# Choosing the experts tile by tile inside the graph layers, a third buffer for late one-hots, and the last projection ahead of the last pair

## The reference

```python
xn = _layernorm(x)
# graph layer: h = xn @ W; agg = segment_sum(norm * h[src], dst) + dinv^2 * h
#              h = layernorm(agg + b) * gamma + beta; relu(0.5 * h + 0.5 * xn)
# attention:   linear attention of all nodes, q = elu(q) + 1, one context for all; projected
x = x + _L0_gnn_ref(xn, ...) + _L0_mix_ref(xn[None], ...)[0]
# experts:     logits = x @ gate_w + gate_b; top 2; softmax of the two; relu(x @ w1 + b1) @ w2 + b2
#              y = x + weighted sum of the two experts; layernorm
x = x + _L0_ffn_ref(_layernorm(x)[None], ...)[0]
return x
```

## Time and profile before

| | us |
|---|---|
| median of 3 runs | 1805.78 |
| lowest and highest of them | 1800.36, 1808.45 |
| the profiled execution | 1800.89 |
| its span | 1799.1 |
| TensorE's matmuls busy | 1490.5 (83%) |
| GpSimd busy | 1065.6 (59%) |
| VectorE busy | 983.1 (55%) |

### The profile page before, as it was taken

How to read it: one execution, slowest core, us unless ns; L and a number is a source line. 1 busy time by engine, 2 the same in 40 slices (tenths; PEclk the granted TensorE clock), 3 DMA queues, 4 the chain that set the end, 5 groups by cost and what they waited for, 6 DMA issues and landing times. The chain is left out here.

```text
span 1799.1 us, 34047 instructions
## 1 busy us (share of the span) xinstructions
PE 1490.5 (83%) x7872; PEld 1211.9 (67%) x7873; DVE 983.1 (55%) x3365; ACT 531.1 (30%) x1463; POOL 1065.6 (59%) x1116
## 2 busy tenths in 40 slices
PE   7999778777978786977887779873499999999987
PEld 4676566565757565755765557652289989988976
DVE  8999466534466453742755347266833333343457
ACT  3444422111211121211211112110055555555523
POOL 2332477777777777777777777760045545545545
PEclk9999879986978898898889979876699999999989
DMA  8010533333333333333333333337432233254266
GB/s 277 28 36 24 164 103 106 106 103 105 104 105 103 104 104 105 102 105 105 103 103 104 105 102 105 104 101 144 114 110 77 72 118 94 73 182 131 70 233 232
DMA packets 105305, 200.76 MB, mean 112 GB/s; under 512 B 24384, under 2 KB 59840, under 8 KB 105248
## 3 DMA queue, kind: packets, MB, share of 16 engines
q0 software_dynamic: 48336, 132.17, 25.3%
q1 hardware_dynamic: 56624, 67.29, 12.2%
q10 hardware_dynamic: 288, 0.66, 0.1%
HBM read 166.44 MB, written 33.60 MB: 111 GB/s over the span
## 5 line engine op out<-in xcount | busy, mean ns | idle before, releaser
L786 POOL DMA_INDIRECT ring<-table,staged x784 | 746.1, 952 | 242.5 <-issue 229.4
L1061 PE MATMUL bank<-ring,hots 128*128 x1372 | 325.0, 392 | 50.3 <-SPq L775 50.3
L1061 PEld LDWEIGHTS bank<-ring,hots 128*128 128x128 f32 x1372 | 266.0, 196 | 100.6 <-issue 63.6
L1458 POOL DMA_INDIRECT got_x<-rows,at_x x114 | 110.2, 967 | 201.9 <-DVE at_x L1576 178.5
L1061 PE MATMUL bank<-ring,late_hots 128*128 x388 | 138.5, 506 | 98.2 <-SPq L775 89.6
L1553 PEld LDWEIGHTS bank<-xT,w 128*128 128x128 f32 x1696 | 207.1, 193 | 15.4 <-issue 10.2
L1553 PE MATMUL bank<-xT,w 128*128 128x128 f32 x1696 | 208.3, 276 | 8.6 <-issue 8.6
L1526 ACT ACTIVATE hT<-bank,b 128x128 f32<-128x128 f32 x424 | 155.7, 367 | 181.4 <-PE bank L1553 156.9
L1561 PE MATMUL bank<-w,hT 128*128 128x256 f32 x848 | 201.1, 380 | 2.3 <-DVE y L1618 2.2
L1061 PEld LDWEIGHTS bank<-ring,late_hots 128*128 128x128 f32 x388 | 90.2, 248 | 140.4 <-issue 126.5
L871 DVE TENSOR_SCALAR hots<-iota_t,edge_l 128x128 f32<-128x128 f32 x686 | 181.8, 363 | 1.8
(11 more groups left out here) (278 smaller groups left out, 2287.4 us busy)
## 6 DMA issues: line engine op xcount, KB each, us to landing
w<-in_w SPq DMA_DIRECT2D x32, 512.0 KB, 4.9
ring<-table,staged POOLq DMA_INDIRECT x784
got<-spread SPq DMA_DIRECT2D x11, 1024.0 KB, 8.1
rows<-xn SPq DMA_DIRECT2D x1, 6272.0 KB, 28.6
out<-out_c SPq DMA_DIRECT2D x12, 512.0 KB, 3.9
xt<-in_x_cols SPq DMA_DIRECT2D x11, 512.0 KB, 3.5
table<-xn SPq DMA_DIRECT2D x6, 896.0 KB, 6.5
x<-in_x SPq DMA_DIRECT2D x4, 896.0 KB, 11.2
```

The costliest lines, as they stand in the source:

```text
L786: pool.indirect_dma_start(out=ring[:, j, :], out_offset=None, in_=a.table, in_offset=bass.IndirectOffsetOnAxis(ap=staged[:, half, col:col ...
L1061: last = nc.tensor.matmul(agg, hot[:, k, :], two[:, k, :], start=False, stop=False)
L1458: pool.indirect_dma_start(out=got[:, n, :], out_offset=None, in_=a.rows, in_offset=bass.IndirectOffsetOnAxis(ap=at[:, n:n + 1], axis=0)).t ...
```

## The change

1. Top two in the layers. In turn t VectorE takes the top two of tile t - 6 (`top_two`, ten operations of 16 columns, behind `x1` and ahead of the wait for the tile's sum), TensorE ranks and counts that tile a turn later in the bank of the gate's product, and VectorE adds the counts so far (`m.run`) to its ranks and writes them over its logits. This is done for tiles 0 to 43 (`ROUTED`). `route` treats the five tiles left: operations of 80 columns, one count matmul and one rank matmul, five chained adds of 16 columns. The one-hots are kept in 16 bits. The shares are worked out behind the places.
2. `late_hots` has a third buffer: a tile's second later pair is built into it without a wait. A third later pair would still wait.
3. The output sum of the last tile (48) is made ahead of its last pair, with its halved input in `cur`, and not in turn 49.
4. Turns 6 and 7 are written out instead of looped. `rows_i`, `xT` and `hT` lie in memory of other tiles, and `places`, `list`, `lists` and `which` are allocated in `moe`.

```diff
+def top_two(dve, c, m, t, score, pick, rest, both):
+    down = m.const[:, C_DOWN:C_DOWN + E]
+    of = tile(m.logits, t, E)
+    for k in range(2):
+        best, one = tile(m.share, t, 2)[:, k:k + 1], tile(m.one[:, k], t, E)
+        c.add(dve.reduce_max(best, of, axis=AX.X))
+        c.wait()
+        settle(dve, m)
+        c.add(dve.scalar_tensor_tensor(score, of, best, down, ALU.is_equal, ALU.mult))
+        c.wait()
+        settle(dve, m)
+        c.add(dve.reduce_max(pick, score, axis=AX.X))
+        c.wait()
+        settle(dve, m)
+        c.add(dve.tensor_scalar(one, down, pick, None, ALU.is_equal))
+        c.wait()
+        settle(dve, m)
+        if k == 0:
+            c.add(dve.scalar_tensor_tensor(rest, one, -3e38, of, ALU.mult, ALU.add))
+            c.wait()
+            settle(dve, m)
+        of = rest
+    return dve.tensor_tensor(both, tile(m.one[:, 0], t, E), tile(m.one[:, 1], t, E), ALU.add)
...
                 with dve.If(end < last):
                     weighted(0, end)
                     with dve.If(end + 1 < last):
-                        with dve.Fori(end + 1, last) as pair:
+                        weighted(2, end + 1)
+                    with dve.If(end + 2 < last):
+                        with dve.Fori(end + 2, last) as pair:
                             dve.wait_ge(freed, pair + CREDIT)
                             settle(dve, m)
                             weighted(0, pair)
...
+                if routed(t, 6):
+                    top_two(dve, Count(dve, chain_top, (t - 6) * CHAIN_TOP, CHAIN_TOP), m, t - 6, score[:], pick[:], rest[:],
+                            m.both[:, n, :]).then_inc(both_ok, 1)
...
+                    if routed(t, 7):
+                        dve.tensor_tensor(tile(m.logits, t - 7, E), rank_ps, m.run[:, n, :], ALU.add)
+                        dve.tensor_tensor(m.run[:, o, :], total_ps, m.run[:, n, :], ALU.add)
...
+                    if routed(t, 7):
+                        pe.wait_ge(both_ok, t - 6)
+                        nc.tensor.matmul(rank_ps, m.tri, m.both[:, 1 - n, :], start=True, stop=True)
+                        done = nc.tensor.matmul(total_ps, m.ones, m.both[:, 1 - n, :], start=True, stop=True)
...
-                if on(t, 1):
...
+                if on(t, 1) and not (isinstance(t, int) and t == LAST + 1):
+                    summed_up(t - 1, 1 - n, tile(m.xn, t - 1))
...
+                    if isinstance(t, int) and t == LAST:
+                        summed_up(t, n, cur[:])
                     pe.wait_ge(late_ok, late + (base + t + 1))
                     settle(pe, m)
                     visit(agg, late_hots[:, n, 1], last)
...
+            nc.tensor.matmul(total_ps, m.ones, m.both[:], start=True, stop=True).then_inc(rank_ok, 1)
+            nc.tensor.matmul(rank_ps, m.tri, m.both[:], start=True, stop=True).then_inc(rank_ok, 1)
```

`summed_up` holds the four steps L1101 to L1108 as they were. In `route` the loop over tiles becomes:

```diff
+            for k in range(LEFT):
+                c.add(dve.tensor_tensor((ran[:, k + 1, :] if k < LEFT - 1 else cnt[:]), run, total_ps[:, k, :], ALU.add))
+                c.wait()
+                run = ran[:, k + 1, :] if k < LEFT - 1 else None
```

More of the change, by code:

```diff
@@ L36 @@
 EARLY = 7
+ROUTED = NT - 5
 BODY = 128
@@ L92, in memory @@
     m.share = sb("share", [P, NT, 2])
[L93 to L96, removed]
+    m.one = sb("one", [P, 2, NT, E], F16)
+    m.both = sb("both", [P, NT - ROUTED, E])
+    m.run = sb("run_e", [P, 2, E])
     m.ident = m.const[:, C_ID:C_ID + P]
@@ L747, in pairs_of @@
             return first, soon, end, late, last, base, ended
[L749 removed]
+        LAST = NT - 1
+        FIRST_TURN, UNROLLED, LAST_TURN = -3, 4, NT + 4
         def turns(turn):
@@ L762, in on, with routed @@
             return not isinstance(t, int) or 0 <= t - back < NT
+        def routed(t, back):
+            return not isinstance(t, int) or 0 <= t - back < ROUTED
         def later(t, least):
@@ L821, in _ @@
             c.add(dve.memset(mv[:], 1.0))
+            c.add(dve.memset(m.run[:], 0.0))
             c.add(dve.memset(var[:], 1.0))
@@ L1062, in visit, with summed_up @@
                 return last
+            def summed_up(t, k, halved):
+                if later(t, 2):
+                    pe.wait_ge(proj_read, t - 1)
+                    settle(pe, m)
+                nc.tensor.matmul(sum_ps[k][:], m.ones[0:1, :], m.vecs[0:1, V_BETA:V_BETA + 2 * D], start=True, stop=False)
+                nc.tensor.matmul(proj_ps[k], m.ident, tile(m.x1, t), start=False, stop=False)
+                pe.wait_ge(xnh_ok, t + 1)
+                settle(pe, m)
+                nc.tensor.matmul(halved_ps[k], m.ident, halved, start=False, stop=False)
+                pe.wait_ge(attT_ok, t + 1)
+                for ch in range(DC):
+                    done = nc.tensor.matmul(proj_ps[k], attT[:, k, ch, :], m.attend[:, ch, :], start=False, stop=(ch == DC - 1))
+                done.then_inc(proj_ok, 1)
             def turn(u, n):
@@ L1162, in moe @@
         SLOTS = 4
+        m.places = ctx.enter_context(nc.sbuf_tensor("places", [P, NT, 2], I32))
+        m.list = ctx.enter_context(nc.sbuf_tensor("list", [P, BLOCKS + 4, 2], I32))
+        m.lists = ctx.enter_context(nc.sbuf_tensor("lists", [1, 2, E], I32))
+        m.which = ctx.enter_context(nc.sbuf_tensor("which", [P, BLOCKS + 4, 2], F32))
         e = Names()
@@ L1204, in route @@
         cnt = sb("cnt", [P, E])
+        ran = sb("ran", [P, LEFT, E])
         nb = sb("nb", [P, E])
@@ L1294, in _ @@
[L1294 to L1303 removed]
+            dve.tensor_tensor(m.both[:], m.one[:, 0, ROUTED:NT, :], m.one[:, 1, ROUTED:NT, :], ALU.add).then_inc(both_ok, 1)
@@ new lines, in _ @@
+            dve.tensor_tensor(gap[:], m.share[:, :, 1], m.share[:, :, 0], ALU.subtract).then_inc(gap_ok, 1)
+            c.add(dve.tensor_copy(ran[:, 0, :], m.run[:, (ROUTED + 7) % 2, :]))
+            dve.wait_ge(rank_ok, 1)
+            run = m.run[:, (ROUTED + 7) % 2, :]
+            here = m.logits
+            for k in range(LEFT):
+                c.add(dve.tensor_tensor((ran[:, k + 1, :] if k < LEFT - 1 else cnt[:]), run, total_ps[:, k, :], ALU.add))
+                c.wait()
+                run = ran[:, k + 1, :] if k < LEFT - 1 else None
@@ L1304, in _ @@
             c.add(dve.tensor_scalar(nb[:], cnt[:], 1.0, float(BLOCK - 1), ALU.max, ALU.add))
+            dve.wait_ge(rank_ok, 2)
+            c.add(dve.tensor_tensor(here[:, ROUTED:NT, :], rank_ps, ran[:], ALU.add))
             c.wait()
@@ L1329, in _ @@
             c.wait()
-            for k, (t0, t1) in enumerate(SPLIT):
-                c.add(dve.tensor_tensor(here[:, t0:t1, :], here[:, t0:t1, :], rank_ps[k][:, 0:t1 - t0, :], ALU.add))
-            c.wait()
             for k in range(2):
-                c.add(dve.tensor_tensor(score[:], here[:], one[k][:], ALU.mult))
+                c.add(dve.tensor_tensor(score[:], here[:], m.one[:, k], ALU.mult))
                 c.wait()
@@ L1339, in _ @@
                 c.wait()
+            dve.wait_ge(eg_ok, 1)
+            c.add(dve.tensor_scalar(gap[:], eg[:], 1.0, None, ALU.add))
+            c.wait()
+            c.add(dve.reciprocal(m.share[:, :, 0], gap[:]))
+            c.wait()
+            dve.tensor_tensor(m.share[:, :, 1], eg[:], m.share[:, :, 0], ALU.mult).then_inc(gates_ok, 1)
             c.add(dve.tensor_single_scalar(part_i[:, 0], m.places[:], P - 1, ALU.bitwise_and))
```

106 lines of the change are left out of this document (45 added, 61 removed).

## The result

The changed kernel takes 1791.47 us (median of four runs, 1790.89 to 1792.06), the kernel before 1807.07 us beside it (1800.36 to 1808.45). The ratio is 0.9921, with a 95% interval of 0.9895 to 0.9947: 0.8% faster. The profiled execution of after took 1790.89 us, span 1789.0, against 1800.89 and 1799.1 of before. So the two profiled executions differ by 10.1 us of span and the medians by 15.6; the profile of before is from the low end of its runs, as the prediction had said, while the runs of after lie within 1.2 us of each other.

The account below looks back on a forecast made before the run. Gather issue on GpSimd bounds the layers; behind the last gather all is serial. -18.2 + 3.3 + 0.3 - 0.5 = -15.1 us: 1785.8 from the profiled 1800.89, 1790 forecast for a median; range 1780 to 1798.

Parts of the forecast that it names:

- What bounds the kernel: Layers: bound by GpSimd's gather issue, 1.26 us a gather; other engines' turns are covered under 20.2 us a tile.
- Part 1: Routing block: top two of five tiles instead of 49, shorter matmul wait, five adds; -18.2 us, between -16.5 and -19.5.
- Part 2: Layers: top two tile by tile, 3.8 us a VectorE turn, making 17.1 us, under 20.2; costs nothing.
- The edge of the cover: VectorE's turn in the layers: new work is covered up to 20.2 - 13.3 = 6.9 us a turn.
- the rival of slow turns: Layers: chained operations at 0.9 us stretch gathers in 44 turns by 2.3 us each, 101 us slower, 1890; chance 0.04.
- The rule on the shared port: Layers: skill's rule that VectorE's two-port operations lock GpSimd out; the trace does not show it, cost below 1 us.
- The lockout rival: Layers: two one-hot operations in each of 44 tiles hold GpSimd 0.17 us each; 15 us come back, 1805; chance 0.04.
- Part 3: Layers: third pair buffer removes VectorE's six waits, 164.8 us; gain taken as -0.5 us (+1.0 to -1.3).
- Part 4: Last tile's projection between its seventh and last pair: the tile's end moves by +3.3 us, nothing comes back.
- the clock falls ahead of the last pairs: Tile 48: after a 2 us wait the seventh pair and projection run at 1.2 GHz, some 3 us more, 1794; chance 0.17.
- The tail and the weights: After routing: last weights lead the first fetch by about 7 us, costed at nothing; rival up to 3 us, 1793, 0.05.

Follow-up runs that it names:

- x_first_3: The changed kernel with the last tile's sum made ahead of all its pairs, on a steady chip: 1785.64 us, 0.99 of the kernel before.
- x_pad: The changed kernel with 352 different source rows behind the padding edges instead of row 0, on a steady chip: 1788.46 us, 0.9914 of the kernel before.
- x_double_2: The changed kernel with each tile's top two worked out twice in the layers, on a steady chip: 1791.55 us, 0.9928 of the kernel before.
- b_again: The kernel before, unchanged, with a profile of its own, on a stalling chip: 2124.44 us, ratio 1.0007.

## Why the prediction came out right, point by point

**What bounds the kernel: right on a steady chip.** VectorE was busy 1068.9 us for 983.1, TensorE 1520.6 for 1490.5, and the last gather started 1.5 us later, where I had forecast 0.5 earlier. That is not fixed either: with the same layers the last gather started at 1209.97 in `x_first_3` and 1209.63 in `x_pad`. On the stalling chips the sentence doesn't hold. There, on one chip, the third buffer alone gave 0.9744 and the kernels with all of the layers' change 0.993 and 0.9947. The buffer is in those too, so what they have beside it costs 36 to 38 us there by the medians (2190.34 and 2191.94 less 2154.43), although their routing block is the shorter one. That the chained operations are what costs is supported by doubling them, another 3% (1.0241 for 0.993 or 0.9947; it has the projection between the pairs, which the others don't).

**Part 1: right in each term.** Forecast -18.2, measured -18.0. The operations of 80 columns start 0.28 us apart on average for 0.27: 1238.45 to 1241.76, 3.3 us for 3.2. The wait for the counts' matmul is 0.8 us (0.7), the five adds end 1.0 us later (1.0), and the shares take 0.9 us in the chain (1.0). The lead of the last weights in the kernel before, which the prediction gives as 26 us, is 27 by its own figures (1272.8 to 1299.8).

**Part 2: right, and the cover is where I put it.** The ten operations take 3.7 us in a turn (746.37 to 750.10) and the two adds 0.2, together 3.9 for 3.8, with the ten in front of a wait of 2.71 us. The edge of the cover, 6.9 us of new work, was right as the point at which VectorE becomes the slowest engine: 7.0 us made a turn of 20.6 on average. Wrong was what follows, in the rival of slow turns and again in what I expected of the doubling. I multiplied the surplus by 44 as if it stretched the gathers, but a surplus first uses up the lead and the ring's depth, and only its rest is paid, once, at the end. The rival's 101 us would rather be some 60: 44 x 2.3 less the 40 us of the ring, by this estimate.

**The rule on the shared port: no trace shows it at work.** With 100 us more of VectorE's work in the layers (612.3 us busy for 511.8 up to the last gather) the 784 gathers took 747.8 us for 746.1, and with them doubled 749.1; in `x_pad`, with the same operations as after, 746.5. The lockout rival's 15 us did not come. The Trainium skill, "SBUF — State Buffer", "SBUF: two separate sides", has GpSimd stopped while VectorE runs an operation in a two-port mode. In which mode these operations ran no row tells, so the runs show only that these operations don't stop these gathers, and not that the rule is wrong.

**Part 3: open in size.** Forecast -0.5. The waits are gone. On a steady chip it can't be told from the rest, and there it was not run alone.

**Part 4: the path right, the size off.** Forecast +3.3, measured +5.3, and the step that failed is the price of the four steps: I took 3.0 us from the full clock. They took 5.4 (1218.06 to 1223.42) at the lower one, behind a wait of 4.81 us and not 1.12, and the seventh pair 0.4 more (1216.19 to 1218.06); it was begun 0.3 us sooner behind the last gather (4.8 for 5.1). This is the rival that I gave 0.17, "the clock falls ahead of the last pairs". It was priced at some 3 us, and 2.4 in the four steps and 0.4 in the pair were seen; its wait of 2 us was an underestimate.

The reason that I gave for it, that TensorE without the stall of tile 46 arrives early, is not borne out. The stall is gone in `x_pad`, `x_double_2` and `x_first_3` too, and there TensorE comes 1.8, 2.0 and 1.6 us ahead of the last gather, near the 1.3 of the kernel before. What sets the changed kernel apart is the tile ahead: there TensorE waited 0.43 us for the last pair of tile 47 and L1117 behind it took 1.12 us (1201.83), while in the other three it waited 1.71 to 2.13 us and that step took 2.07 (1203.18 in `x_double_2`). From the closing matmul of tile 47 to the first pair of tile 48 it is 4.8 us in the changed kernel (1200.34 to 1205.14), 9.2 in `x_pad` and 9.1 in `x_double_2`, and tile 47 closes 11 us ahead of the last gather in all three. So it was a low clock one tile earlier that made TensorE late in these and spared them the long wait.

The projection between the pairs met the low clock in the changed kernel's trace, in neither `x_pad` nor `x_double_2`, so it is an event of timing. In `x_double_2`, at the full clock, the last pair starts 3.9 us behind the seventh for 1.5 in the kernel before: +2.4, less than the forecast's 3.3. The row at 1189.91 that the rival leans on stands behind 7.3 us in which TensorE waited for ScalarE (L1035); a wait of 3.12 us for landed rows, with the lower clock behind it, lies ahead of that, at 1172.85.

**The tail and the weights: right.** SyncE's last row of the weights ends at 1280.95, 8.6 us ahead of the first fetch (about 7 forecast), and no fetch waits. The list loop is 0.6 us longer.

**The sum came out at the forecast with help.** On the profiled basis I forecast 1785.8 and got 1790.9: 5.1 us too low (1.5 + 0.5 of gathers, 2.0 of part 4, 0.2 of part 1, 0.8 behind). For the median I added the 4.9 us by which the profile of before lay under its median, and got 1790.7 for 1791.47. The runs of after don't have that spread. Their median is 0.6 us above their profiled one. So an error of 5.1 us and one of 4.3 the other way met, and that the median came out within 1 us is luck. Why the runs of before spread over 8 us and those of after, `x_pad` and `x_first_3` over 1 to 2 us (`x_double_2`: 5) was not found. The stalls of the earlier trace rows that the third buffer removes are the obvious candidate; the run that would have tested it fell on a stalling chip.

## What to carry to other kernels

An engine's slack per turn is the point from which it becomes the slowest, not the point from which its work costs time: multiply the surplus by the turns, take off the depth of the buffer between it and the bound, and look for what is left behind the last turn. Work that is to fill a wait has to stand ahead of the wait; how much that is worth depends on how long the wait is when the engine gets there. At a like arrival the same four matmuls cost 1.1 us more behind the wait than ahead of it; with an early arrival, a wait of 4.81 us and the low clock, the place behind it cost 5.3 us. So look at how early the engine comes in several executions, and not in one. Before a forecast for a median is made from one profiled execution, ask whether the spread that separates the two will outlive the change.

## What the runs showed of the hardware

- **Two kinds of chips.** The same program took 1804 to 1807 us on some and 2125 to 2205 us on others. In `b_again` 277 of the 316 us more lie in the layers, 1266 us from first to last gather instead of 989, with a gather at 952 ns in both. The waits there stand ahead of instructions of TensorE, VectorE and ScalarE and are put down to "issue" or "remote"; what is behind them isn't to be seen in any trace here.
- **Many reads of one row land late.** With 352 padding edges that read one row the last gather landed after 4.6 and 4.2 us, with distinct rows after 2.7.
- **The clock fell after 4.81 us of waiting** and not after waits of 1.12 (kernel before) or 0.59 us (`x_double_2`) in the same place; L1117 then took 2.07 us instead of 1.12. The Trainium skill, "TensorE: Matmul & The Clock Gate", "HAM oscillation", has a wait for a transfer bring the slow clock; these rows agree.
